# Four reordered steps in a pipelined matmul kernel: a gate transposition placed behind v, u's second half a row further on, the last two results written in four parts

## The chip, the cores and the metric

The kernel runs on one core of one Trainium2 chip. The metric is the device time of one execution in microseconds (us). Before the change the median of three runs is 1119.69 us (1118.13 to 1120.51). The profiled execution took 1119.37 us, and its span, from the first to the last instruction, is 1117.6 us. A difference of less than 0.2% (2.24 us) is about what this kernel's measurement can't tell from no change.

## The reference

Input x is 128 samples of 64 channels by 1024 positions, fp32. Two layers are added to x, one after the other:

- Layer 0: a small network on `cond_128` gives each sample a softmax over 8 experts, so a 64x64 matrix per sample (`agg_w`) and a bias. `x = x + ((agg_w @ x + agg_b) @ (A @ B.T).T + bias)`, with A and B of rank 128.
- Layer 1: a grouped convolution over the 1024 positions (4 groups of 16 channels, 9 taps) with a bias per sample and channel gives y. Then `x = x + y @ W_up.T + delta`, where four gate logits `y @ gate_w.T + expert_bias` choose one expert per row (argmax), and delta is that expert's rank 8 product.

## The kernel before

**Tiles.** Work goes over 32 supertiles (`NS`) of 4 samples, each of two tiles of 128 rows (`NT` = 64), in a software pipeline: the body `for it in range(1, NS)` multiplies supertile `it` by W_up while it prepares `it+1` and `it+2`. Each engine (TensorE is `pe`, ScalarE `act`, VectorE `dve`, the DMA queue of SyncE `sp`) has an order of its own, written out by hand, and they meet at semaphores. fp32 numbers are split into a high and a low fp32r half, and each product is three matmuls (high x high, high x low, low x high).

**Rows.** TensorE's pass has 44 rows, `row(it, n // 4, n % 4)`: 11 blocks of 4 rows with 3 matmuls each (lines 1351 to 1400). Blocks "s" have 384 columns, blocks "c" 292 (the four gate logits, the 32 rank products of the experts and 256 columns of W_up). Between the rows stand the units for the coming supertiles, at fixed places n (lines 1579 to 1622):

- `unit_u(s, h)`: 12 matmuls, x transposed times B, half h at a time, into PSUM tile F[2]. It waits for the low half of x from VectorE (`txl`, line 799). The second half stands behind row 9.
- `unit_tu`: two transpositions of u, behind row 11. ScalarE copies u out of PSUM before it (`ut`) and behind it (`tuu`).
- `unit_v`: u times the samples' matrices, in plain fp32, behind row 13. VectorE adds the bias (`vv`), ScalarE and VectorE split v (`vhi`, `vlo`).
- `unit_p(s, g)` and `unit_c(s, g)`: the convolution. p for g = 0 and 1 is written into PSUM tile M[2], behind rows 15 and 18; ScalarE adds the bias and spreads it (`pc`), and c adds to it.
- `unit_o`: layer 0's last product, four parts, rows 22 to 27.
- `unit_zt(t)`: one transposition (96x128) of the chosen expert's products, `zs`. For the first tile of a supertile (t even) it goes into M[2], behind row 21, for the second into G, behind row 38. ScalarE copies the result into `zst` (`zt`, line 589), and `unit_dl` multiplies it (rows 24 and 28, and row 41). `zs` is made by VectorE in seven small operations (`zc`, lines 961 to 983) once block 2, rows 8 to 11, is complete.

**Who waits for what around the change.** ScalarE's order in a pass is ... h4, ut, tuu, vhi, pc(0), pc(1), bias(0), zt, bias(1) ...; VectorE's is S4, l12, txl, lC, xs, zc, vv, vlo, addU, lB, ty(0) .... In the order of SyncE's queue a pass stores tiles 2it-1 and 2it-2, loads two tiles, copies `Xr`, then loads `xTr` when u's second half is done (line 274), loads `agg` when v is done (296) and `agb` when `vv` is done (287), and so on.

**The end.** `v_f` counts VectorE's six final additions of a supertile, in this order: f11 and fG (rows 0 to 4 of the first tile's 8), f22 and fH (rows 3 to 7 of the second), f21 (rows 0 to 2 of the second), f12 (rows 5 to 7 of the first). A `store` (line 350) writes a tile of 516 KB in one transfer, after `v_f` 5 for the second tile, after 6 for the first. The same `store` closes the kernel (lines 410 and 411).

Of the kernel before, what the change touches and what calls it, by code (L numbers as in the profile page):

```python
# [11 lines left out]
NS = 32  # L12
NT = 64
# [10 lines left out]
XR = 6  # L24
# [8 lines left out]
def adaln_ffn(nc, xT, xP, mlp, wkx, Bd, Ad, biasP, ccT, fsX, Td, Wcd, Wsd, Ld, ebias, out):  # L33
# [10 lines left out]
    with ctx:  # L44
# [3 lines left out]
        def sb(name, shape, dt=fp32):  # L48
            size = 4
            for n in shape[1:]:  # L50
                size *= n
            place[name] = place[""]
            place[""] += (size + 31) // 32 * 32
            assert place[""] <= nc.sbuf_usable_end, (name, place[""], nc.sbuf_usable_end)
            return nc.alloc_sbuf_tensor_at(name, shape, dt, offset=place[name])
# [42 lines left out]
        x1 = sb("x1", [128, XR, 8, 129])  # L98
# [64 lines left out]
        def sem(name):  # L163
            return ctx.enter_context(nc.semaphore(name))
# [9 lines left out]
        d_st = [sem(f"d_st{j}") for j in range(XR)]  # L174
# [4 lines left out]
        a_txh, a_u, a_tu, a_vh, a_xr, a_xs, a_bi, a_pc, a_yh, a_cp, a_zt = (  # L179
            sem(n) for n in ("a_txh", "a_u", "a_tu", "a_vh", "a_xr", "a_xs", "a_bi", "a_pc", "a_yh", "a_cp", "a_zt"))  # L180
        v_mlp, v_wk, v_ag, v_agb, v_b, v_cs, v_a, v_t, v_cb, v_l, v_wc, v_tt, v_w = (
            sem(n) for n in ("v_mlp", "v_wk", "v_ag", "v_agb", "v_b", "v_cs", "v_a", "v_t", "v_cb", "v_l", "v_wc", "v_tt", "v_w"))
        v_txl, v_v, v_vl, v_x1, v_d, v_xr, v_xs, v_ty, v_s, v_yl, v_ux, v_z, v_f = (
            sem(n) for n in ("v_txl", "v_v", "v_vl", "v_x1", "v_d", "v_xr", "v_xs", "v_ty", "v_s", "v_yl", "v_ux", "v_z", "v_f"))
# [76 lines left out]
        def _(sp):  # L261
# [88 lines left out]
            def store(t):  # L350
                s, q = t // 2, t % 2
                sp.wait_ge(v_f, 6 * s + (6 if q == 0 else 5))
                sp.dma_start(out[t], x1[:, t % XR]).then_inc(d_st[t % XR], 16)

            sp.dma_start(pack, mlp).then_inc(d_mlp, 16)
            sp.dma_start(wkr[:, :], wkx).then_inc(d_wk, 16)
            load_xT(0, 0)
# [41 lines left out]
            for it in range(1, NS):  # L399
# [7 lines left out]
                load_agb(it + 3)  # L407
                rx(it + 2, 0)
                load_xT(it + 3, 1)
            store(NT - 1)  # L410
            store(NT - 2)
            for j in range(XR):
                sp.wait_ge(d_st[j], 16 * ((NT - 1 - j) // XR + 1))

        @block.gpsimd
        def _(pool):
# [19 lines left out]
        def _(act):  # L436
            def copy(dst, src):
                return act.activation(dst, src, ACT.Copy)  # L438
# [21 lines left out]
            def tuu(s):  # L460
                if s >= NS:
                    return
                act.wait_ge(p_tu, s + 1)
                copy(u[:, :], F[2][:, 0:256]).then_inc(a_tu, 1)

            def vhi(s):
                if s >= NS:
                    return
                act.wait_ge(v_v, s + 1)
                copy(vh[:, :, :, :, :].rearrange("p q g b n -> p b (q g) n"),  # L470
                     v[:, :].rearrange("p (b g n) -> p b g n", b=4, g=4)).then_inc(a_vh, 1)
# [92 lines left out]
            def h4(s):  # L564
                act.wait_ge(v_s, 4 * s + 4)
                copy(yh[:, 6], yr[:, 6]).then_inc(a_yh, 1)
# [22 lines left out]
            def zt(t):  # L589
                act.wait_ge(p_zt, t + 1)  # L590
                copy(zst[:, :], (M[2] if t % 2 == 0 else G)[0:96, 0:128]).then_inc(a_zt, 1)
# [174 lines left out]
            for it in range(1, NS):  # L766
                txh(it + 2, 1)
                cpGH(it)
                xs(it + 1, 0)
                cpAB(it)  # L770
                h4(it)
                ut(it + 2)
                tuu(it + 2)
                vhi(it + 2)
                pc(it + 1, 0)
                pc(it + 1, 1)
                bias(it + 2, 0)
                zt(2 * it)
                bias(it + 2, 1)
                xsr(it + 1)  # L780
                bias(it + 2, 2)
                xsd(it + 1)
                bias(it + 2, 3)
                hA(it + 1)
                txh(it + 3, 0)
                pc(it + 1, 2)
                cpCD(it)
                pc(it + 1, 3)
                zt(2 * it + 1)
                hB(it + 1)  # L790
                hC(it + 1)
# [463 lines left out]
        def _(pe):  # L1255
# [25 lines left out]
            def unit_v(s):  # L1281
                if s >= NS:
                    return
                pe.wait_ge(a_tu, s + 1)
                pe.wait_ge(d_gg, 32 * s + 64 + 32 * min(s, 1))
                pe.matmul(F[2][:, 0:128], u[:, 0:128], agg[:, 0, :], start=True, stop=True)  # L1286
                pe.matmul(F[2][:, 128:256], u[:, 128:256], agg[:, 1, :], start=True, stop=True).then_inc(p_v, 1)  # L1287
# [16 lines left out]
            def unit_p(s, g):  # L1304
                if s >= NS:
                    return
                if g % 2 == 0:
                    if s == 0:
                        pe.wait_ge(v_xr, g // 2 + 1)
                    else:  # L1310
                        pe.wait_ge(v_xs, 2 * s + g // 2 + 1)
                if s == 0:
                    if g == 0:
                        pe.wait_ge(v_t, 2)
                        pe.wait_ge(v_cs, 1)
                    if g == 1:
                        pe.wait_ge(v_cb, 4)
                    if g > 1:
                        pe.wait_ge(a_pc, 1 if g == 2 else 3)
                elif g == 0:  # L1320
                    if s == 1:
                        pe.wait_ge(a_pc, 4)
                    else:
                        pe.wait_ge(v_f, 6 * (s - 2) + 5)
                elif g == 2:
                    pe.wait_ge(v_v, min(s + 2, NS))
                else:
                    pe.wait_ge(a_pc, 4 * s + g)
                b0 = 4 * (g % 2)
                q = g // 2  # L1330
                for n_, (w, m) in enumerate(((Th, XH(s, q)), (Tl, XH(s, q)), (Th, XL(s, q)))):
                    last = pe.matmul(pbank(s, g)[:, 0:256], w[:, g, 2, :], m[:, 2, b0:b0 + 4, :].rearrange("p b i -> p (b i)"),  # L1332
                                     start=n_ == 0, stop=n_ == 2)
                last.then_inc(p_p, 1)
# [67 lines left out]
            def unit_zt(t):  # L1402
                pe.wait_ge(v_z, 7 * t + 7)
                s = t // 2
                if t % 2 == 0:
                    pe.wait_ge(a_pc, 4 * min(s + 1, NS - 1) + (2 if s + 1 < NS else 4))
                    if s > 0:
                        pe.wait_ge(v_f, 6 * (s - 1) + 5)
                else:
                    pe.wait_ge(v_f, 6 * s + 2)  # L1410
                pe.transpose((M[2] if t % 2 == 0 else G)[0:96, 0:128], zs[:, :], ident[:, :]).then_inc(p_zt, 1)
# [167 lines left out]
            for it in range(1, NS):  # L1579
                for n in range(44):  # L1580
                    row(it, n // 4, n % 4)
                    if n == 9:
                        unit_u(it + 2, 1)
                    if n == 11:
                        unit_tu(it + 2)
                    if n == 13:
                        unit_v(it + 2)
                    if n == 15:
                        unit_p(it + 1, 0)
                    if n == 18:  # L1590
                        unit_c(it + 1, 0)
                        unit_p(it + 1, 1)
                    if n == 21:
                        unit_c(it + 1, 1)
                        unit_zt(2 * it)
                    if n == 22:
                        unit_o(it + 2, 0)
                    if n == 23:
                        unit_o(it + 2, 1)
                    if n == 24:  # L1600
                        unit_dl(2 * it, 0)
                        unit_dl(2 * it, 1)
                    if n == 25:
                        unit_o(it + 2, 2)
                    if n == 27:
                        unit_o(it + 2, 3)
                    if n == 28:
                        unit_dl(2 * it, 2)
                    if n == 30:
                        unit_p(it + 1, 2)  # L1610
                    if n == 34:
                        unit_c(it + 1, 2)
                        unit_p(it + 1, 3)
                    if n == 37:
                        unit_c(it + 1, 3)
                    if n == 38:
                        unit_zt(2 * it + 1)
                    if n == 40:
                        unit_u(it + 3, 0)
                    if n == 41:  # L1620
                        for c in (2, 1, 0):
                            unit_dl(2 * it + 1, c)
# [61 lines left out]
```

## Time and profile before

| | |
|---|---|
| median of 3 runs | 1119.69 us |
| profiled execution | 1119.37 us |
| its span | 1117.6 us |
| TensorE matmul busy | 1085.9 us, 97% of the span |
| VectorE busy | 911.1 us, 82% |
| ScalarE busy | 613.5 us, 55% |
| mean granted TensorE clock | 0.990 |
| DMA, mean over the span | 136 GB/s |

A busy share tells how much of the span an engine had an instruction under way. A matmul's record is longer than the time that it keeps the next one waiting, since they are pipelined; the distance between two starts is what one costs. A weight load (PEld) comes ahead of its matmul, beside the matmul before it. Each row of a timeline is: start in us from the span's start, duration in us, engine, line of the kernel, operation, destination and sources, shape, and in brackets the idle time before it and what ended that. The clock is a share of full speed.

### The profile page before, as it was taken

To read this page: it belongs to the slowest core of one execution; us is meant where nothing else is said; L and a number is where in the kernel's file an instruction comes from. 1 tells how busy PE (TensorE), PEld (TensorE's weight loads), DVE (VectorE), ACT (ScalarE), POOL (GpSimd) and SP (SyncE) were. 2 spreads that over 40 slices of the span, in tenths; PEclk is the share of its full clock that TensorE was granted. 3 is DMA by queue.
4 is the path that set the end of the run, shared out by engine and by line. 5 is a ranking of instruction groups with operands and counts; after the bars stand their busy time and mean duration, and the time that the engine had idled before them with its cause. 6 is when DMAs were issued, how large, how long until landed. Compare 5 with 4: busy or idle time off the path is not lost.

```text
span 1117.6 us, 19137 instructions
## 1 busy us (share of the span) xinstructions
PE 1085.9 (97%) x7020; PEld 1052.2 (94%) x7020; DVE 911.1 (82%) x1670; ACT 613.5 (55%) x1243; POOL 4.5 (0%) x17
## 2 busy tenths in 40 slices
PE   6599999999999999999999999999999999999998
PEld 4478999999999999999999999999999999999998
DVE  5899788888878878878888887887887887888774
ACT  5675555545555555555655555554555555555541
POOL 1000000000000000000000000000000000000000
PEclk9699999999999999999999999999999999999999
DMA  8844455554445554445554454555445555544321
GB/s 317 268 71 135 117 119 151 149 141 138 116 106 153 143 159 128 122 120 128 146 153 138 137 119 104 154 146 151 132 118 114 142 144 156 132 136 121 83 58 76
DMA packets 118048, 152.03 MB, mean 136 GB/s; under 512 B 21836, under 2 KB 91980, under 8 KB 117804
## 3 DMA queue, kind: packets, MB, share of 16 engines
q1 hardware_dynamic: 116516, 148.49, 49.4%
q10 hardware_dynamic: 1440, 2.33, 0.6%
q8 instruction: 56, 0.92, 0.3%
q14 instruction: 36, 0.29, 0.1%
HBM read 80.87 MB, written 35.95 MB: 105 GB/s over the span
## 4 chain that ended last, share of the span: by engine, by line
PE 91%; DVE 4%; DMA 2%; issue 1%; SPq 1%; ACT 1%; DVEq 0%; ACTq 0%
PE M L1398 41%; PE H L1398 9%; PE G L1398 9%; PE F L1347 8%; PE F L1299 7%; PE F L1269 3%; PE F L1271 3%; PE F L1270 3%; PE F L1332 2%; PE M L1332 2%; PE M L1429 2%; DMA Br<-in_Bd_dram 1%; PE F L1287 1%; PE F L1286 1%; DMA Xr<-x 1%
## 5 line engine op out<-in xcount | busy, mean ns | idle before, releaser
L1398 PE MATMUL M<-Wsh,yh 128*128 128x384 f32 x896 | 313.1, 349 | 0.4 <-DVE yl L939 0.4
L1398 PE MATMUL M<-Wsh,yl 128*128 128x384 f32 x896 | 302.9, 338 | 0.0
L1398 PE MATMUL M<-Wsl,yh 128*128 128x384 f32 x896 | 302.9, 338 | 0.0
L888 DVE STREAM_TRANSPOSE yr<-F 128x512 f32<-128x512 f32 x126 | 90.2, 716 | 128.9 <-PE F L1347 80.7
L1398 PEld LDWEIGHTS M<-Wsh,yh 128*128 128x128 f32 x896 | 168.6, 188 | 5.6 <-DVE yl L939 0.7
L1398 PEld LDWEIGHTS M<-Wsl,yh 128*128 128x128 f32 x896 | 168.9, 188 | 2.8
L1398 PEld LDWEIGHTS M<-Wsh,yl 128*128 128x128 f32 x896 | 168.2, 188 | 0.0
L438 ACT ACTIVATE yh<-yr 128x1024 fp32r<-128x1024 f32 (+1 forms) x127 | 120.2, 946 | 53.6 <-DVE yr L903 41.4
L539 ACT ACTIVATE F<-F,cbX 128x128 f32<-128x128 f32 x248 | 69.0, 341 | 94.9 <-PE F L1332 94.1
L539 ACT ACTIVATE F<-M,cbX 128x128 f32<-128x128 f32 x260 | 72.4, 342 | 66.1 <-PE M L1332 66.0
L438 ACT ACTIVATE xTh<-xTr 128x1024 fp32r<-128x1024 f32 x64 | 67.3, 1052 | 61.7 <-DMA xTr<-in_xT_dram 61.7
L438 ACT ACTIVATE F<-biasb 128x512 f32<-128x512 f32 x124 | 74.1, 598 | 25.2 <-DVE yr L888 19.1
L831 DVE TENSOR_TENSOR x<-F,x 128x512 f32<-128x512 f32 x124 | 82.4, 685 | 3.9 <-PE F L1299 0.2
L799 DVE TENSOR_TENSOR xTl<-xTr,xTh 128x1024 fp32r<-128x1024 f32 x64 | 77.8, 1218 | 0.4 <-ACT xTh L438 0.3
L1398 PE MATMUL G<-Wch,yh 128*128 128x292 f32 x256 | 76.3, 298 | 1.1 <-ACT H L438 0.8
L1398 PE MATMUL H<-Wcl,yh 128*128 128x292 f32 x256 | 76.2, 297 | 0.0
L1398 PE MATMUL G<-Wcl,yh 128*128 128x292 f32 x256 | 76.1, 297 | 0.0
L1398 PE MATMUL G<-Wch,yl 128*128 128x292 f32 x256 | 76.1, 297 | 0.0
L1398 PE MATMUL H<-Wch,yl 128*128 128x292 f32 x256 | 76.1, 297 | 0.0
L1398 PE MATMUL H<-Wch,yh 128*128 128x292 f32 x256 | 75.9, 297 | 0.0
L865 DVE TENSOR_TENSOR Xl<-Xd,Xh 128x1024 fp32r<-128x1024 f32 x62 | 75.5, 1218 | 0.0
L1347 PE MATMUL F<-Xh,Th 128*128 128x256 f32 x256 | 73.7, 288 | 1.1 <-DVE Xl L873 0.9
(206 smaller groups left out, 2478.0 us busy)
## 6 DMA issues: line engine op xcount, KB each, us to landing
x<-in_xP_dram SPq DMA_DIRECT2D x64, 516.0 KB, 4.2
out_dram<-x SPq DMA_DIRECT2D x64, 516.0 KB, 3.5
xTr<-in_xT_dram SPq DMA_DIRECT2D x64, 512.0 KB, 4.0
Xr<-x SPq DMA_DIRECT2D x508, 64.5 KB, 2.5
agb<-agb_scratch SPq DMA_DIRECT2D x31, 128.0 KB, 3.5
agg_scratch<-stage SPq DMA_DIRECT2D x1, 2048.0 KB, 9.1
agg<-agg_scratch SPq DMA_DIRECT2D x60, 32.0 KB, 3.3
Wsr<-in_Wsd_dram SPq DMA_DIRECT2D x2, 768.0 KB, 11.0
```

The costliest lines, as they stand in the source:

```text
L438: return act.activation(dst, src, ACT.Copy)
L539: last = act.activation(F[g % 2][:, 128 * b:128 * b + 128].rearrange("p (e i) -> p e i", e=2), pbank(s, g)[:, 64 * b:64 * b + 64].unsqueez ...
L799: dve.tensor_tensor(xl(s, h)[:, :, :], xsrc(s, h)[:, :, :], xh(s, h)[:, :, :].bitcast(fp32), ALU.subtract).then_inc(v_txl, 1)
L831: dve.tensor_tensor(dst, obank(s, i)[:, :].rearrange("p (c a) -> p c a", c=4), dst, ALU.add).then_inc(v_x1, 1)
L865: dve.tensor_tensor(l_[:, 0:2], d_[:, 0:2], h_[:, 0:2].bitcast(fp32), ALU.subtract).then_inc(v_xs, 1)
L888: dve.transpose(dst.rearrange("p j k m -> p (j k) m").rearrange("p (k r) (g b n) -> p g b k r n", r=2, g=2, b=4)[:, g % 2], F[g % 2][:, :] ...
L1269: pe.matmul(F[2][:, 0:256], Bh[:, 4 * h + c, :], xh(s, h)[:, c, :], start=first, stop=False)
L1270: pe.matmul(F[2][:, 0:256], Bh[:, 4 * h + c, :], xl(s, h)[:, c, :], start=False, stop=False)
L1299: last = pe.matmul(obank(s, i)[:, :], w[:, q].rearrange("p g b n -> p (g b n)"), m[:, 4 * h:4 * h + 4, :].rearrange("p c a -> p (c a)"), s ...
L1332: last = pe.matmul(pbank(s, g)[:, 0:256], w[:, g, 2, :], m[:, 2, b0:b0 + 4, :].rearrange("p b i -> p (b i)"), start=n_ == 0, stop=n_ == 2)
L1347: last = pe.matmul(dst[:, e], w[:, g, e, :], m[:, e, b0:b0 + 4, :], start=False, stop=n_ == 2, skip_group_check=True)
L1398: last = pe.matmul(dst, w[:, y, k, :], m, start=fresh and n_ == 0, stop=k == 3 and n_ == 2, skip_group_check=True)
```

## The change

On TensorE u's second half moves from behind row 9 to behind row 10, u's transposition from behind row 11 to behind row 12, v from behind row 13 to behind row 14. `unit_zt(2 * it)`, which was behind row 21, now follows v directly. So it stands ahead of `unit_p(it + 1, 0)`, which writes the same PSUM tile M[2]; it no longer waits for ScalarE's `pc`, and `unit_p(s, 0)` now waits for ScalarE's copy of that transposition (`a_zt`, 2s-1) in place of `v_f`. On ScalarE `zt(2 * it)` moves from behind `bias(it + 2, 0)` to between `tuu` and `vhi`. On SyncE the two last stores become four: rows 0 to 4 of tile 62 after fG (`v_f` 2), rows 3 to 7 of tile 63 after fH (4), rows 0 to 2 of tile 63 after f21 (5), rows 5 to 7 of tile 62 after f12 (6).

```diff
@@ -351,6 +351,10 @@
                 s, q = t // 2, t % 2
                 sp.wait_ge(v_f, 6 * s + (6 if q == 0 else 5))
                 sp.dma_start(out[t], x1[:, t % XR]).then_inc(d_st[t % XR], 16)
+
+            def last_store(t, r0, r1, n):
+                sp.wait_ge(v_f, 6 * (NS - 1) + n)
+                sp.dma_start(out[t][:, r0:r1, :], x1[:, t % XR, r0:r1, :]).then_inc(d_st[t % XR], 16)
 
             sp.dma_start(pack, mlp).then_inc(d_mlp, 16)
             sp.dma_start(wkr[:, :], wkx).then_inc(d_wk, 16)
@@ -407,10 +411,13 @@
                 load_agb(it + 3)
                 rx(it + 2, 0)
                 load_xT(it + 3, 1)
-            store(NT - 1)
-            store(NT - 2)
+
+            last_store(NT - 2, 0, 5, 2)
+            last_store(NT - 1, 3, 8, 4)
+            last_store(NT - 1, 0, 3, 5)
+            last_store(NT - 2, 5, 8, 6)
             for j in range(XR):
-                sp.wait_ge(d_st[j], 16 * ((NT - 1 - j) // XR + 1))
+                sp.wait_ge(d_st[j], 16 * ((NT - 1 - j) // XR + (2 if j in ((NT - 1) % XR, (NT - 2) % XR) else 1)))
 
         @block.gpsimd
         def _(pool):
@@ -771,11 +778,11 @@
                 h4(it)
                 ut(it + 2)
                 tuu(it + 2)
+                zt(2 * it)
                 vhi(it + 2)
                 pc(it + 1, 0)
                 pc(it + 1, 1)
                 bias(it + 2, 0)
-                zt(2 * it)
                 bias(it + 2, 1)
                 xsr(it + 1)
                 bias(it + 2, 2)
@@ -1321,7 +1328,7 @@
                     if s == 1:
                         pe.wait_ge(a_pc, 4)
                     else:
-                        pe.wait_ge(v_f, 6 * (s - 2) + 5)
+                        pe.wait_ge(a_zt, 2 * s - 1)
                 elif g == 2:
                     pe.wait_ge(v_v, min(s + 2, NS))
                 else:
@@ -1402,10 +1409,10 @@
             def unit_zt(t):
                 pe.wait_ge(v_z, 7 * t + 7)
                 s = t // 2
-                if t % 2 == 0:
-                    pe.wait_ge(a_pc, 4 * min(s + 1, NS - 1) + (2 if s + 1 < NS else 4))
-                    if s > 0:
-                        pe.wait_ge(v_f, 6 * (s - 1) + 5)
+                if t == 0:
+                    pe.wait_ge(a_pc, 6)
+                elif t % 2 == 0:
+                    pe.wait_ge(v_f, 6 * (s - 1) + 5)
                 else:
                     pe.wait_ge(v_f, 6 * s + 2)
                 pe.transpose((M[2] if t % 2 == 0 else G)[0:96, 0:128], zs[:, :], ident[:, :]).then_inc(p_zt, 1)
@@ -1579,12 +1586,13 @@
             for it in range(1, NS):
                 for n in range(44):
                     row(it, n // 4, n % 4)
-                    if n == 9:
+                    if n == 10:
                         unit_u(it + 2, 1)
-                    if n == 11:
+                    if n == 12:
                         unit_tu(it + 2)
-                    if n == 13:
+                    if n == 14:
                         unit_v(it + 2)
+                        unit_zt(2 * it)
                     if n == 15:
                         unit_p(it + 1, 0)
                     if n == 18:
@@ -1592,7 +1600,6 @@
                         unit_p(it + 1, 1)
                     if n == 21:
                         unit_c(it + 1, 1)
-                        unit_zt(2 * it)
                     if n == 22:
                         unit_o(it + 2, 0)
                     if n == 23:
```

## Rows read from the trace of the kernel before

**Rows 1.** The page, part 1: busy time of each engine.

```profile
PE 1085.9 (97%) x7020; PEld 1052.2 (94%) x7020; DVE 911.1 (82%) x1670; ACT 613.5 (55%) x1243; POOL 4.5 (0%) x17
```

**Rows 2.** Windows of TensorE: stretch, length, PE busy (x), PEclk, DMA share, GB/s.

```profile
1000.00:1050.00 50.00, 50.00 (x330) 1.00 0.49 132
```

**Rows 3.** Timeline of one pass: u's first half's start, then its second half's.

```profile
696.20 0.28 PE L1269 MATMUL F<-xTh,Bh 128*128 128x256 f32 x1
696.32 0.28 PE L1270 MATMUL F<-xTl,Bh 128*128 128x256 f32 x1
...
702.86 1.22 DVE L799 TENSOR_TENSOR xTl<-xTr,xTh 128x1024 fp32r<-128x1024 f32 x1
...
704.14 0.19 PEld L1269 LDWEIGHTS F<-xTh,Bh 128*128 128x128 f32 x1
704.20 0.33 PE L1269 MATMUL F<-xTh,Bh 128*128 128x256 f32 x1
...
704.37 0.28 PE L1270 MATMUL F<-xTl,Bh 128*128 128x256 f32 x1
```

**Rows 4.** The same pass's timeline: v, the end of zc, the next row.

```profile
707.76 0.38 PE L1286 MATMUL F<-agg,u 128*128 128x128 f32 x2
...
708.22 0.19 DVE L983 TENSOR_TENSOR zs<-zm,zs 128x32 fp32r<-128x32 f32 x1
...
708.38 0.34 PE L1398 MATMUL M<-Wsl,yh 128*128 128x384 f32 x1
```

**Rows 5.** The same pass's timeline: zt, ScalarE's copy, the row behind, the next unit.

```profile
714.58 0.27 PE L1411 MATMUL M<-ident,zs 128*96 128x128 f32 x1
...
714.87 0.34 PE L1398 MATMUL M<-Wsl,yh 128*128 128x384 f32 x1
...
714.89 0.27 ACT L438 ACTIVATE zst<-M 96x128 fp32r<-96x128 f32 x1 [0.53 <-PE M L1411]
...
715.23 0.40 PE L1299 MATMUL F<-Ah,vh 128*128 128x512 f32 x1
```

**Rows 6.** Timeline: three places where TensorE waits for another engine's copy.

```profile
26.73 0.38 ACT L438 ACTIVATE u<-F 128x256 f32<-128x256 f32 x1 [4.33 <-PE F L1271]
...
27.16 0.14 PEld L1278 LDWEIGHTS F<-ident,u 128*128 128x128 f32 x1 [0.68 <-ACT u L438]
...
106.90 0.40 ACT L438 ACTIVATE H<-G 128x292 f32<-128x292 f32 x1
...
107.41 0.19 PEld L1398 LDWEIGHTS G<-Wch,yh 128*128 128x128 f32 x1 [1.06 <-DVE yl L933]
...
1063.96 0.19 PEld L1398 LDWEIGHTS M<-Wsh,yh 128*128 128x128 f32 x1 [0.25 <-DVE x L1014]
...
1064.24 0.34 PE L1398 MATMUL M<-Wsl,yh 128*128 128x384 f32 x1
```

**Rows 7.** Timeline of the last two passes: row 15's start and zc's end.

```profile
1069.80 0.34 PE L1398 MATMUL M<-Wsh,yh 128*128 128x384 f32 x1
...
1070.57 0.19 DVE L983 TENSOR_TENSOR zs<-zm,zs 128x32 fp32r<-128x32 f32 x1
...
1097.16 0.19 DVE L983 TENSOR_TENSOR zs<-zm,zs 128x32 fp32r<-128x32 f32 x1
1097.20 0.34 PE L1398 MATMUL M<-Wsh,yh 128*128 128x384 f32 x1
```

**Rows 8.** Timeline of the end: f12 and the issue of the last two stores.

```profile
1113.14 0.56 DVE L1014 TENSOR_TENSOR x<-M,x 128x384 f32<-128x384 f32 x1
1113.16 0.90 SPq L353 DMA_DIRECT2D out_dram<-x  x2
```

**Rows 9.** Line 353 in 1110 to 1118 us: issue to landing of the last two stores.

```profile
DMA to landing us min/median/max: 2.7/3.0/3.4
```

**Rows 10.** Windows at the end: length, PE, PEld, DVE, ACT, POOL, PEclk, DMA share, GB/s.

```profile
1114.00:1116.40 2.40, 0.00 (x0) 0.00 (x0) 0.00 (x0) 0.00 (x0) 0.00 (x0) 1.00 1.02 409
```

**Rows 11.** The page, part 3: SyncE's DMA queue: packets, MB, share of 16 engines.

```profile
q1 hardware_dynamic: 116516, 148.49, 49.4%
```

## Prediction

> **What bounds the kernel now.** I first read the page's busy shares: TensorE 97% of the span, VectorE 82%, ScalarE 55% [rows 1]. Then the span cut into stretches of 50 us: from 150 us on TensorE is busy throughout and granted the full clock, 2.4 GHz [rows 2]. So the middle of the kernel costs what TensorE's queue costs, and only two things change the time there: matmuls added or removed (the change does neither), and gaps too short to be listed as idle, since the records of pipelined matmuls overlap. These show in the timeline as a distance between two starts above the usual one. Last I read the end, where TensorE is done and the stores are left.
>
> **u's second half a row later: -1.45 us.** In the first half, the second matmul starts 0.12 us after the first. In the second half it starts 0.17 us after, and its weight load is at 704.14, just behind VectorE's xTl, which ends at 702.86 + 1.22 = 704.08 [rows 3]. So TensorE loses 0.05 us here for VectorE. One row more ahead of u is some 0.4 us, far more than that, and VectorE's order up to xTl is not touched, so the gap closes. u's second half exists in 29 passes (it = 1 to 29): 29 x 0.05 = 1.45 us. The bounds are none and 0.06 each, 0 to -1.75.
>
> u's transposition and v keep their distances to u or gain (rows 11 and 12 between them now, 10 and 11 before), so the copies ut and tuu are in time. What is queued behind them comes later: SyncE's load of the next xTr by 0.4 us, those of agg and agb, VectorE's vv and vlo and ScalarE's vhi by 0.5 us. Cover: xTr is copied only at the end of the pass, agg and agb are read in the next one, and vlo has until row 22. Behind vlo, addU has until row 20 and lB until row 24, several rows of 0.5 us later. The copies of Xr that follow in SyncE's queue wait for later additions anyway. I cost these at nothing; if addU's cover were gone, row 20 would wait for what it lacks, in each pass.
>
> **The transposition itself: nothing.** It is only moved. From its start to the second matmul of the row behind are 0.29 us; take off a row matmul's 0.18 and it costs 0.11 [rows 5]. Would it be cheaper right behind v, another plain fp32 product? v is four passes of 128 columns, and takes 708.38 - 707.76 - 0.18 = 0.44 us, again 0.11 each [rows 4]. Passes side by side are no cheaper than one alone, which excludes a gain; and none is dearer, which excludes a loss.
>
> **Does zt wait for zc? In the middle no, in the last two passes yes: +1.4 us.** The new zt starts when row 14 and v are done. Row 14 comes first now (3 x 0.175 = 0.525), then v (0.445): 707.76 + 0.97 = 708.73, less the 0.05 that u no longer loses, 708.68. zs is complete at 708.22 + 0.19 = 708.41 [rows 4], so it is in time by about 0.1 us, with 0.15 to spare for the handover and the weight load. In pass 30 there is no u, tu or v left to fill the rows, but VectorE's work ahead of zc is the same: zc ends at 1070.57 + 0.19 = 1070.76, while zt's place, the start of row 15, is at 1069.80 [rows 7]. With 0.05 for the handover and 0.10 for the weight load (below) zt starts at 1070.91: +1.1 us. In pass 31 zc ends at 1097.35 and row 15 starts at 1097.20 [rows 7]: +0.3. Behind both places TensorE has no slack that could take it up. Bounds: with a quicker load 0.95 and 0.2, and with zt's 0.11 lost once more because a later wait keeps its place, 1.2 and 0.4; 1.15 to 1.6.
>
> **p now waits for ScalarE's copy of zt: +2.7 us.** This is the wait that the change adds. Behind zt stands one row, then unit_p(it+1, 0), which must not overwrite M[2] before ScalarE has copied. Today's zt gives the times: the copy starts 0.31 us after zt's start (714.89 - 714.58) and takes 0.27, so it ends at 0.58; the unit behind the next row starts at 715.23, 0.65 after zt [rows 5]. ScalarE is free (tuu is long done). Where TensorE waited for such a copy into SBUF, its weight load came at 27.16, 0.05 behind 26.73 + 0.38 [rows 6]: 0.63. And a matmul whose load was held starts about 0.10 later: the row at 1063.96 has its second matmul at 1064.24, so the first counts as from 1064.24 - 0.18 = 1064.06 [rows 6]. That makes 0.73 instead of 0.65, or by the row lengths (0.11 + 0.525) instead of 0.64: a hold of 0.08 to 0.10, I take 0.09. There are 30 (it = 1 to 30): 2.7 us. Lower bound: nothing, if only the matmul waits and its weights are loaded ahead, since 0.63 is before 0.65. Upper bound: the load at 107.41 came 0.11 behind ScalarE's copy (106.90 + 0.40) [rows 6], which makes the hold 0.15 and the sum 4.5. The nearest row is the 0.05 of a copy to SBUF, as zst is. Queued behind p are all later rows; ScalarE's pc and TensorE's c follow p at unchanged distances. The Trainium skill, in TensorE: Matmul & The Clock Gate, "Step-by-step: what each phase is for", says that TensorE pulls weight loads ahead of matmuls under way, so that the next weights load beside them; by that the hold would be nothing and the whole 2.7 us less. The row at 1063.96 speaks against it where a wait is in front: that wait protects a PSUM tile only, and the load still came behind it.
>
> **The four last stores: -1.0 us.** Now f21's store goes out at 1113.16 and f12's at about 1113.72 [rows 8]. The latter lands 3.4 us after its issue (the longer of the two) [rows 9], at 1117.1. The two hold 2 x 128 x 4128 bytes, 1.06 MB, which at 409 GB/s [rows 10] take 2.6 us; so 1.4 us are left between the first issue and the landing that no data fills. A lone store agrees: the shorter of the two lands after 2.7 us [rows 9], 1.3 of data and 1.4 beside. After the change 5 rows of tile 62 leave some 10 us earlier, under the rows. Behind fH, done about 0.5 us before 1113.14, 5 rows of tile 63 follow, then 3 rows (0.2 MB) after f21 and 3 after f12: 11 rows of 16, 0.73 MB, 1.8 us. From an issue at 1112.7, with the 1.4, the end is 1115.9: -1.2. Shorter packets cost more: the queue's 116516 packets of 1.27 KB took 0.494 x 1117.6 x 16 = 8833 us, 76 ns each [rows 11], against 161 ns for 4128 bytes at 409 GB/s [rows 10]; on the line between these a packet of 1548 bytes takes 84 ns and one of 2580 bytes 115, eight per engine: 0.9 + 0.7 + 0.7 = 2.3 us, end at 1116.4: -0.7. I take -1.0. The issues on SyncE's queue, about 0.35 us each, fit between the additions. Bounds: 0 (completion is what takes the time) and -1.5 (the last part alone, 1113.72 + 1.4 + 0.5). By the Trainium skill, DMA: Bandwidth & Descriptors, "Anatomy of one DMA", a transfer costs some 2.0 us fixed plus its bytes at 436 GB/s, an estimate of 2.45 us for the last part by which this term would be -0.95; that page's "Bandwidth" also advises batches of 1 MiB or more, against splitting.
>
> **The sum:** -1.45 + 1.4 + 2.7 - 1.0 = +1.65 us. Against the profiled execution's 1119.37 (1.8 us more than its span) that is 1121.0 us. This execution stands 0.3 us under the median of 1119.69.
>
> **The rivals.**
> - *p is not held.* Weights are loaded ahead and the copy is in time. For it: 0.63 against 0.65. Against it: the load behind 1063.96. 1121.0 - 2.7 = 1118.3, still no change that can be told.
> - *The handover from ScalarE takes 0.11 us, and the kernel gets slower.* Place: the same p, in 30 passes; price 0.15 each, 4.5 instead of 2.7: 1122.8 us. It decides from a hold of about 0.11 each, where the sum passes +2.24. For it: 107.41. Against: that copy writes PSUM, and 27.16.
> - *The stores bring nothing,* completion bound: 1122.0.
> - *zt comes too early in each pass,* its slack of 0.1 us being eaten: with 0.1 more in 29 passes, 1123.9. Against it: zc's time repeats to a few hundredths.
>
> **How the numbers follow.** My forecast 0.55, p not held 0.14, a longer handover 0.17, stores without gain 0.08, zt too early 0.06. The range goes from p not held to the longer handover: 1118.3 to 1122.8 us. Over 0.2% faster (2.24 us, about what a measurement of this kernel can tell) needs p not held and both other gains at their best: 0.06. Slower takes the handover, half of the last two, and the forecast's upper edge: 0.28. The rest, 0.66, is no change.
>
> **What would show it.** In the changed profile: u's second half with 0.12 between its first two matmuls; the weight load of p at zt's start + 0.63, p's matmul 0.08 to 0.10 late, and M L1332 waiting on ScalarE's zst; TensorE waiting some 1.1 us before zt near 1070 us and 0.3 near 1097; SyncE's last issue landing under 3 us. Wrong would be: p's load beside the row ahead of it, zt waiting in middle passes, or row 20 waiting for addU.

## The result and the profile after

The changed kernel takes 1123.01 us, the median of 7 runs (1122.29 to 1125.26), beside 1119.45 us for the kernel before (7 runs, 1117.78 to 1120.51): ratio 1.0037, 95% interval 1.0026 to 1.0049. It is slower by 3 to 5.5 us. The forecast was 1121.0 us with a range to 1122.8. The profiled execution took 1122.56 us, its span is 1120.8 us.

The page, part 1, of the changed kernel (before: [rows 1]):

```profile
PE 1089.4 (97%) x7020; PEld 1047.7 (93%) x7020; DVE 912.2 (81%) x1670; ACT 613.5 (55%) x1243; POOL 4.3 (0%) x17
```

The shares hardly differ. What differs is the length of a pass: zt of the second tile stands behind row 38 in both kernels, so the distance between two of them is one pass. Timeline of TensorE, that transposition at the start and the end of the same four passes, the kernel before:

```profile
728.12 0.27 PE L1411 MATMUL G<-ident,zs 128*96 128x128 f32 x1
...
860.46 0.28 PE L1411 MATMUL G<-ident,zs 128*96 128x128 f32 x1
```

and the changed kernel:

```profile
728.73 0.27 PE L1418 MATMUL G<-ident,zs 128*96 128x128 f32 x1
...
861.55 0.27 PE L1418 MATMUL G<-ident,zs 128*96 128x128 f32 x1
```

132.34 / 4 = 33.085 us before, 132.82 / 4 = 33.205 after: +0.12 us a pass. The forecast, -0.05 for u and +0.09 for p, was +0.04. Timeline of one pass of the changed kernel, u's second half first, then zt, its copy, and p:

```profile
705.14 0.28 PE L1276 MATMUL F<-xTh,Bh 128*128 128x256 f32 x1
...
705.26 0.28 PE L1277 MATMUL F<-xTl,Bh 128*128 128x256 f32 x1
...
708.80 0.19 DVE L990 TENSOR_TENSOR zs<-zm,zs 128x32 fp32r<-128x32 f32 x1
...
709.09 0.13 PEld L1418 LDWEIGHTS M<-ident,zs 128*96 128x96 f32 x1
...
709.20 0.27 PE L1418 MATMUL M<-ident,zs 128*96 128x128 f32 x1
...
709.51 0.27 ACT L445 ACTIVATE zst<-M 96x128 fp32r<-96x128 f32 x1 [1.23 <-PE M L1418]
...
709.90 0.19 PEld L1339 LDWEIGHTS M<-Xh,Th 128*128 128x128 f32 x1 [0.22 <-issue]
...
709.93 0.36 PE L1339 MATMUL M<-Xh,Th 128*128 128x256 f32 x1
...
710.12 0.28 PE L1339 MATMUL M<-Xh,Tl 128*128 128x256 f32 x1
```

u's second matmul comes 0.12 us after the first: the gap of [rows 3] is closed. zs is ready at 708.99, and zt's weights load at 709.09, beside v and 0.11 ahead of zt, at v's own pace, so zt waits for nothing. The copy starts 0.31 us after zt and ends at 709.78, 0.58 after it, as in [rows 5]. But p's weight load comes only at 709.90, 0.12 us behind that end where I took 0.05, and p's second matmul shows it starting as from 710.12 - 0.12 = 710.00, 0.80 after zt in place of 0.64. The hold is 0.16 to 0.17 us.

The last two passes, timeline of zc's end and zt (before: [rows 7]):

```profile
1072.98 0.19 DVE L990 TENSOR_TENSOR zs<-zm,zs 128x32 fp32r<-128x32 f32 x1
...
1073.22 0.12 PEld L1418 LDWEIGHTS M<-ident,zs 128*96 128x96 f32 x1 [1.18 <-DVE zs L990]
...
1100.91 0.19 DVE L990 TENSOR_TENSOR zs<-zm,zs 128x32 fp32r<-128x32 f32 x1
...
1101.16 0.12 PEld L1418 LDWEIGHTS M<-ident,zs 128*96 128x96 f32 x1 [0.37 <-DVE zs L990]
```

zt waits for zc in both. It has two waits too, but here the late one (for zs) stands first, and the load comes 0.05 and 0.06 behind zs (1073.22 - 1073.17, 1101.16 - 1101.10). By the distance of the second tiles' transpositions the two passes take 29.16 and 23.15 us, before 27.81 and 22.91: +1.6 us.

The end, timeline of f12 and the last three issues, then line 357's issue to landing for them, then two windows (columns as in [rows 10]):

```profile
1116.68 1.36 SPq L357 DMA_DIRECT2D out_dram<-x  x3
...
1117.12 0.56 DVE L1021 TENSOR_TENSOR x<-M,x 128x384 f32<-128x384 f32 x1
```

```profile
DMA to landing us min/median/max: 2.2/2.5/2.6
```

```profile
1118.00:1119.00 1.00, 0.00 (x0) 0.00 (x0) 0.00 (x0) 0.00 (x0) 0.00 (x0) 1.00 1.02 378
1119.00:1120.00 1.00, 0.00 (x0) 0.00 (x0) 0.00 (x0) 0.00 (x0) 0.00 (x0) 1.00 0.46 166
```

The last part, 194 KB, lands within 2.6 us of its issue, where the whole tile took 3.4 [rows 9], and the shorter packets run at 378 GB/s in the full stretch shown, not 409 [rows 10]. From the last transposition (1109.66 before, 1113.66 after) to the end of the span are 7.94 us before and 7.14 after: -0.8 us.

The ledger: 29 passes x 0.12 = +3.5, last two passes +1.6, the end -0.8: +4.3 us. The ratio says +4.1, the difference of the medians is 3.6. Two things are not in this ledger, and both vary from execution to execution: the start, since the second tiles' first transposition comes at 96.55 us in this trace and at 98.64 in the one before (96.5 to 98.7 in the twelve traces of this case), and a few longer passes, +1.6 us in this trace and +0.2 before. So the two spans differ by only 3.2 us, and the pass is a better measure than the span.

**Three passes were longer still**, 34.00, 33.40 and 33.80 us. Timeline of ScalarE in the first:

```profile
303.68 1.06 ACT L445 ACTIVATE xTh<-xTr 128x1024 fp32r<-128x1024 f32 x1 [3.27 <-DMA xTr<-in_xT_dram]
304.64 0.39 ACT L445 ACTIVATE H<-G 128x292 f32<-128x292 f32 x1
```

xTr landed late; behind the copy of it on ScalarE stands the copy of G into H, and row 8 waits for that. The DMA view of that stretch (298.80 to 304.00 us) shows an instruction packet among the loads, and the pass before (265.60 to 270.80) shows none:

```profile
q1 hardware_dynamic: 361, 1.36, 69.9%
q8 instruction: 1, 0.02, 1.1%
...
xTr<-in_xT_dram SPq DMA_DIRECT2D x1, 512.0 KB, 4.8
```

```profile
q1 hardware_dynamic: 371, 1.40, 73.7%
...
xTr<-in_xT_dram SPq DMA_DIRECT2D x1, 512.0 KB, 3.6
```

Whether these passes belong to the change is taken up below.

### The profile page after: what moved, and what is told of

It reads as the page before. It is cut to its first block, busy times and chain, and to the rows that moved or that the text cites. A ratio compares the mean times of both kernels' runs of the same rounds, so it can differ in the third digit from the quotient of the medians.

```text
span 1120.8 us, 19139 instructions
## 1 busy us (share of the span) xinstructions
PE 1089.4 (97%) x7020; PEld 1047.7 (93%) x7020; DVE 912.2 (81%) x1670; ACT 613.5 (55%) x1243; POOL 4.3 (0%) x17
## 4 chain that ended last, share of the span: by engine, by line
PE 91%; DVE 5%; DMA 1%; issue 1%; SPq 1%; ACT 1%; DVEq 0%; ACTq 0%
PE M L1405 40%; PE H L1405 9%; PE G L1405 8%; PE F L1354 8%; PE F L1306 7%; PE F L1278 3%; PE F L1276 3%; PE F L1277 3%; PE M L1339 2%; PE F L1339 2%; PE M L1436 2%; DMA xTr<-in_xT_dram 1%; PE F L1294 1%; PE F L1293 1%; DVE wks L1123 0%
```

## The experiments

The theory (A): the move of zt is the whole loss, by p's hold and by zt's wait in the last two passes; u's row and the stores gain what was forecast. Its rival (B): u and v a row later send SyncE's loads later and lose something there. "Before" is each time the kernel before, run on the same chip as the kernels that it is compared with: 1118.48 us for the first four, 1119.19 for the next four, 1118.64 for the last two.

### zt back behind row 21

```diff
                     if n == 14:
                         unit_v(it + 2)
-                        unit_zt(2 * it)
...
                     if n == 21:
                         unit_c(it + 1, 1)
+                        unit_zt(2 * it)
```

and on ScalarE behind bias(0), with the old waits.

> The changed kernel with the even transposition zt back behind row 21 on TensorE and behind bias(0) on ScalarE, with its old waits; u, its transposition, v and the four last stores stay as changed. Theory A (the loss is the zt move: p(it+1,0) held 0.17 us by ScalarE's copy in 30 passes, zt waiting 1.2 us for zc in the last two): the kernel loses all of that, so the steady pass falls from 33.20 to 33.08 - 0.05 = 33.03 us and the time to 1119.4 - 1.5 - 0.8 = 1117.1 us. Rival B (part of the loss comes from u and v a row later, which send SyncE's loads later, so that the xTr load lands late in some passes and holds row 8): passes of 33.2 to 34 us stay, time 1118 to 1119.5.

Measured: 1115.79 us, ratio 0.9978 (0.9969 to 0.9987), faster than before by 1.5 to 3.5 us. Timeline, the same four passes:

```profile
725.51 0.27 PE L1418 MATMUL G<-ident,zs 128*96 128x128 f32 x1
...
857.63 0.27 PE L1418 MATMUL G<-ident,zs 128*96 128x128 f32 x1
```

132.12 / 4 = 33.03 us, 0.055 under the kernel before and 0.175 under the changed one. The last two passes are back at 27.83 and 22.90. Rival B falls: u and v stand a row later here too, and no pass but the first is over 0.1 us longer than the rest. Nor is the load of xTr that row 8 depends on sent later by the change: in all twelve traces it goes out 2.76 to 2.79 us after the second tile's transposition.

### The four stores alone

```diff
-            store(NT - 1)
-            store(NT - 2)
+            last_store(NT - 2, 0, 5, 2)
+            last_store(NT - 1, 3, 8, 4)
+            last_store(NT - 1, 0, 3, 5)
+            last_store(NT - 2, 5, 8, 6)
```

> The kernel before with the four last stores alone. Theory A: the end from TensorE's last transposition to the last instruction shortens from 7.94 to 7.14 us as in the changed kernel, everything else as before: 1119.4 - 0.8 = 1118.6 us. Rival (the end's time is completion of the last transfer, whatever its size): no change, 1119.4.

Measured: 1118.05 us, ratio 0.9996 (0.9987 to 1.0005). The runs alone can't tell 0.8 us from nothing. In the trace the last transposition is at 1107.45 and the span ends at 1114.4: 6.95 us, against 7.94 before, with passes of 33.07 to 33.11. Over all traces this stretch is 7.93 to 7.99 us in the four kernels with two stores and 6.82 to 7.14 in the eight with four parts, on the mean 6.94: the gain is 0.8 to 1.1 us, mostly 1.0. The first experiment less this one is u's move alone: 33.085 - 33.03 = 0.055 us a pass, 1.6 us.

### zt into G

```diff
-                pe.transpose((M[2] if t % 2 == 0 else G)[0:96, 0:128], zs[:, :], ident[:, :]).then_inc(p_zt, 1)
+                pe.transpose((G[0:96, 292:420] if t % 2 == 0 else G[0:96, 0:128]), zs[:, :], ident[:, :]).then_inc(p_zt, 1)
...
-                        pe.wait_ge(a_zt, 2 * s - 1)
+                        pe.wait_ge(v_f, 6 * (s - 2) + 5)
```

ScalarE copies from there. The output of this kernel is wrong: the transposition now stands between the rows that sum into G and the product that is added to that sum (`unit_dl`, row 24), and what it does to the sum was not followed up. The instructions are the same in number and size as in the changed kernel, so it serves for the times alone.

> The changed kernel with the even transposition written into free columns of PSUM tile G in place of M[2], so that p(it+1,0) doesn't wait for ScalarE's copy (it waits for v_f as before). zt stays right behind v. Theory A: p's weight load comes in the row ahead of it again, 0.17 us less in 30 passes: 1123.0 - 5.0 = 1118.0 us, steady pass 33.03 to 33.05 us. Rival C (what holds p is not the copy but something that follows zt, v and one row, such as the wait instruction itself): p's load still about 0.07 us late, steady pass 33.1 to 33.2, time over 1120.

Measured: 1117.43 us, ratio 0.9993 (0.9984 to 1.0002). Timeline of one pass, zt, its copy, p's weight load:

```profile
708.12 0.27 PE L1418 MATMUL G<-ident,zs 128*96 128x128 f32 x1
...
708.43 0.27 ACT L445 ACTIVATE zst<-G 96x128 fp32r<-96x128 f32 x1 [1.23 <-PE G L1418]
...
708.58 0.19 PEld L1339 LDWEIGHTS M<-Xh,Th 128*128 128x128 f32 x1
708.75 0.28 PE L1339 MATMUL M<-Xh,Th 128*128 128x256 f32 x1
```

The load goes beside the row ahead, while the copy still runs, and p starts 0.63 us after zt. The pass is 32.98 to 33.05 us, three late ones aside; the last two, where zt still waits for zc, are 29.01 and 23.15. So it is the wait for the copy that holds p, and zt right behind v costs nothing in the middle passes. The Trainium skill, TensorE: Matmul & The Clock Gate, "Step-by-step: what each phase is for", has weight loads pulled ahead of running matmuls; this trace agrees (0.17 us ahead) where the wait is long met. The changed kernel's trace shows that a late wait keeps the load behind it.

### The order of p's two waits

Why 0.12 us behind the copy, and 0.05 at [rows 6], first pair? p has two waits, for xs (long past) and then for the copy. The load behind u's copy has one. So has the load at 1063.96, the third place of [rows 6]. What it waits for is not a copy but the addition of VectorE below, which ends at 1063.91, so the load is 0.05 behind. The load at 107.41, 0.11 behind its copy, has two again, and the late one is second (lines 1368 and 1369).

```profile
1063.36 0.55 DVE L1014 TENSOR_TENSOR x<-M,x 128x384 f32<-128x384 f32 x1
```

```diff
+                if g == 0 and s > 1:
+                    pe.wait_ge(a_zt, 2 * s - 1)
                 if g % 2 == 0:
...
                     if s == 1:
                         pe.wait_ge(a_pc, 4)
-                    else:
-                        pe.wait_ge(a_zt, 2 * s - 1)
```

> The changed kernel with the two waits ahead of unit_p(s, 0) in the other order: first for ScalarE's copy of zt (the late one), then for v_xs (long past). The weight load came 0.12 us behind the end of the copy in the changed kernel, but 0.05 us behind it where TensorE waits for one thing only (u's copy). Theory D (the handover is longer when the late wait is the second of two): load 0.05 to 0.06 us behind the copy, hold 0.10 instead of 0.17, 30 x 0.07 = 2.1 us less, 1120.9 us. Rival E (0.12 us belongs to this copy of ScalarE): no change, 1123.0 us.

Measured: 1120.49 us, ratio 1.0018 (1.0007 to 1.0030). Timeline:

```profile
743.93 0.27 PE L1418 MATMUL M<-ident,zs 128*96 128x128 f32 x1
...
744.24 0.27 ACT L445 ACTIVATE zst<-M 96x128 fp32r<-96x128 f32 x1 [1.23 <-PE M L1418]
...
744.57 0.19 PEld L1339 LDWEIGHTS M<-Xh,Th 128*128 128x128 f32 x1 [0.16 <-ACT zst L445]
```

The copy ends at 744.51, the load comes 0.06 behind. The pass is 33.12 us (33.09 to 33.14, three late ones aside), 0.09 less than the changed kernel's. Nothing but the order of two waits was changed. Theory D holds here; the hold that is left is 0.10 to 0.11, about the size that I had forecast.

### The last two passes alone

```diff
+                        if it < NS - 2:
+                            unit_zt(2 * it)
...
                         unit_c(it + 1, 1)
+                        if it >= NS - 2:
+                            unit_zt(2 * it)
```

The same on ScalarE, with the old waits where zt stands at its old place.

> The changed kernel, but in the last two passes (it = 30 and 31) the even transposition stands behind row 21 again, with its old waits. Theory A: the last two passes fall from 29.16 and 23.15 us back to 27.83 and 22.90 (1.6 us together), the other passes stay at 33.20 to 33.21: 1.6 us below the changed kernel run beside it. Rival (the last two passes are long because of p's hold or of the late VectorE chain, wherever zt stands): 28.9 or more and 23.1.

Measured: 1122.64 us, ratio 1.0022 (1.0012 to 1.0032). By the trace as theory A has it: last passes 27.80 and 22.90 us, the undisturbed others 33.13 to 33.21, 33.19 in the middle. By the times the step is not resolved: the changed kernel, run beside it (below), took 1122.73. Five passes of this trace are 0.3 to 0.6 us longer, 2.2 us together, each with late xTr, which hides the step.

### A met wait ahead, and behind

Does D hold for VectorE's results, and at another place? In the kernel before, at u's second half:

```diff
+                if s > 2 and h == 1:
+                    pe.wait_ge(v_v, s)
                 pe.wait_ge(v_txl, 2 * s + h + 1)
```

> The kernel before, with a wait that is long met (for v_v, of the pass before) put ahead of the late wait for VectorE's xTl at u's second half, in 29 passes. Nothing else changes. Theory D (a late wait that stands second hands over 0.06 us later, whatever engine it waits for): the weight load moves from 0.06 to 0.12 us behind xTl's end, u's hold grows from 0.05 to 0.11, steady pass 33.15 us, 29 x 0.06 = 1.7 us slower. Rival E (only ScalarE's copies hand over late): no change, 33.09.

> The same added wait, but behind the late one. Theory D: as the kernel before, steady pass 33.09 us, load 0.06 us behind xTl's end. Rival F (each further wait costs TensorE some 0.06 us where it is held, in whatever order): 33.15 us as with the wait ahead.

Measured: ahead 1123.16 us, ratio 1.0032 (1.0023 to 1.0042); behind 1120.38 us, ratio 1.0008 (0.9998 to 1.0018). Timelines of xTl and u's load, ahead:

```profile
704.90 1.23 DVE L799 TENSOR_TENSOR xTl<-xTr,xTh 128x1024 fp32r<-128x1024 f32 x1 [0.48 <-ACT xTh L438]
...
706.24 0.19 PEld L1271 LDWEIGHTS F<-xTh,Bh 128*128 128x128 f32 x1
```

and behind:

```profile
703.31 1.22 DVE L799 TENSOR_TENSOR xTl<-xTr,xTh 128x1024 fp32r<-128x1024 f32 x1
...
704.58 0.19 PEld L1271 LDWEIGHTS F<-xTh,Bh 128*128 128x128 f32 x1
```

0.11 us (706.24 - 706.13) against 0.05 (704.58 - 704.53), and so in all 28 steady passes of the two traces (0.11 to 0.12 against 0.04 to 0.05). The undisturbed passes are 33.16 us in the middle (33.12 to 33.18) against 33.10 (33.06 to 33.11). D holds for VectorE too: E and F fall. Of the loss of the kernel with the wait ahead, 2.6 to 4.7 us by the ratio, 29 x 0.07 = 2.0 us is this steady part. The forecast of 1.7 us left out the late passes: they make 4.2 us in its trace and 0.2 in the trace before.

### The changed kernel again

> The changed kernel once more, for a second trace and beside the kernels of this call. Theory A: steady pass 33.20 to 33.21 us, last two 29.16 and 23.15. The passes in which xTr lands late and holds row 8 (three of 29 in the first trace, 1.4 us) are either chance (other passes or none here) or belong to the kernel (the same three again).

Measured: 1122.73 us, ratio 1.0029 (1.0018 to 1.0040); pass 33.20 us, last two 29.16 and 23.16. The passes it = 2 and 3 were 0.1 and 0.5 us longer, none of the first trace's three (it = 7, 19, 27). So whether one of those is late changes from execution to execution of the same kernel. Which passes can be late does not, as the account of the late passes below shows.

### Two met waits ahead

As the met wait ahead, with a second one, for `v_vl`.

> The kernel before with two long met waits (for v_v and v_vl of the pass before) ahead of the late wait for xTl at u's second half. Theory D1 (only the last wait goes with the weight load itself, and a held one behind others hands over later by one fixed step): as with one met wait, load 0.11 us behind xTl's end, steady pass 33.15 us. Theory D2 (each wait ahead adds its own 0.06 us): load 0.17 behind, 33.21 us.

Measured: 1121.90 us, ratio 1.0028 (1.0013 to 1.0044). xTl ends at 706.60 in the pass looked at and the load comes at 706.72, 0.12 behind; undisturbed passes are 33.12 to 33.17 us. That is theory D1: the step is one of 0.06 us, with two met waits ahead as with one. Four passes of this trace were over 0.4 us longer, again with late xTr, which is why the loss, 1.5 to 4.9 us by the ratio, can be above the 2 us that the step alone makes.

### A kernel that beats both

zt back behind row 21 as in the first experiment, and at row 8:

```diff
-                    pe.wait_ge(v_yl, 5 * s + 2)
                     pe.wait_ge(a_cp, 3 * s + 1)
+                    pe.wait_ge(v_yl, 5 * s + 2)
```

> The changed kernel with zt back behind row 21, and the two waits ahead of block 2 (row 8) exchanged, so that the one that is late when xTr lands late (ScalarE's copy of G into H) comes first. Theory D: steady pass 33.03 us, as with zt back alone, and 0.07 us less in each of the few passes that wait there: 2.5 to 3 us under the kernel before, 1116.3 us if that takes 1119. Rival: the gain seen with zt back alone was that chip's, under 1 us here.

Measured: 1115.61 us, ratio 0.9971 (0.9961 to 0.9982), 2.0 to 4.4 us under the kernel before. Passes are 32.99 to 33.07 us, but for three of 33.5 to 33.9 with late xTr. So late passes come with zt at its old place as well. Timeline of row 8 in one of them, the copy of G into H and the load behind it:

```profile
304.54 0.40 ACT L445 ACTIVATE H<-G 128x292 f32<-128x292 f32 x1
...
304.99 0.19 PEld L1405 LDWEIGHTS G<-Wch,yh 128*128 128x128 f32 x1 [0.61 <-ACT H L445]
```

The load comes 0.05 behind the copy, and 0.05 to 0.06 in each of the four passes of this trace in which it stands idle for it. With the waits in the old order it is 0.10 to 0.12 in every such pass of the other eleven traces (the 107.41 of [rows 6] is one). So D holds at a third place, and for a copy into PSUM. It is worth 4 x 0.06 = 0.2 us here, too little for the times: the first experiment has 0.9978 (0.9969 to 0.9987) without it.

## Why the prediction was wrong

- **u's row: right.** -0.05 a pass forecast, -0.055 shown (33.09 to 33.03), 1.6 us.
- **zt itself, and zt right behind v: right.** It costs the same there, and waits for nothing in the middle passes (third experiment: 33.03 us a pass, as with zt at its old place).
- **zt in the last two passes: right.** +1.4 and p's hold of 0.09 forecast, +1.6 measured. In the third experiment, where p isn't held, zt's waits alone are 29.01 - 27.83 + 23.15 - 22.90 = +1.4. The fifth takes all of it away in the trace.
- **The stores: right.** -1.0 forecast, -0.8 to -1.1 in the traces, too little for the runs to tell.
- **p's hold: the term that was mis-sized.** The mechanism was as described: the copy 0.58 us after zt, the weight load kept behind the wait, the matmul 0.10 after its load. What failed is "the nearest row is the 0.05 of a copy to SBUF". It measured 0.12, the hold 0.17 instead of 0.09, and the sum 30 x 0.17 = 5.0 us instead of 2.7. I chose between the two rows of [rows 6] by where the copy writes. That is not what matters: the copy into PSUM of the second row hands over in 0.05 too once its wait stands first (the last experiment). What matters is whether a met wait stands ahead of the late one, and p's late one is the second. Exchanging two lines brings back 0.06 us of handover, and 0.09 a pass. The rival with 0.11, given a chance of 0.17, was the case, and at 1122.8 its time was 0.2 us under the median. What in the engine makes the order of the waits matter, no run here shows.

With the hold at 5.0 us the sum is -1.45 + 1.4 + 5.0 - 1.0 = +3.95, against +4.1 by the ratio. The range ended where that rival's time stood, with nothing beyond it for the runs' own spread.

The late passes were not in the forecast. They are in traces of both orders of zt, and small ones in the trace before (33.22 and 33.18 us); between none and five to an execution cost over 0.3 us each, up to 1.1. There are 27 of these in the twelve traces, the first pass aside, and their places are not chance: each is a pass it = 3, 7, 11 and so on, every fourth, or, in the three kernels with an added wait, 24 or 28. All 27 had an instruction packet in the stretch between xTr's issue and the copy of it; of the passes without one, none was over 0.2 us late. But another 32 passes had such a packet and lost 0.2 us at most. So the packet's place goes with the program, and whether it costs anything changes from one execution to the next. That the packet is the cause was not tested.

## What to carry to other kernels

When one instruction waits for several things, put the wait that comes last in time first in the program: on TensorE here that was worth 0.06 to 0.09 us each time, some 2 us over a kernel of 30 passes. A transposition moved ahead of the next user of its PSUM tile turns a wait that was long met into one that is late by as much as the copy, the handover and the held weight load together exceed the rows between them; count those three before moving it. And look at the passes in which the pipeline runs empty: what covers a producer in the middle (u, v and their copies) is not there at the end.

## What the runs showed of the hardware

- TensorE's weight load follows the end of the work that it waits for by 0.05 to 0.06 us when that wait is alone or first, and by 0.10 to 0.12 when one or two long met waits stand ahead of it; for ScalarE's results (p and row 8) and VectorE's (u's second half) alike.
- A held weight load starts its matmul 0.10 to 0.11 us later, so a hold begins before any idle time shows: in the changed kernel the profile gives none for p's matmul, only "0.22 <-issue" ahead of the load.
- The last three parts, one of 323 KB and two of 194, landed 2.2 to 2.6 us after their issue, the first of the two whole tiles of 516 KB after 2.7 [rows 9]. The Trainium skill, DMA: Bandwidth & Descriptors, "Anatomy of one DMA", gives some 2.0 us plus the bytes at 436 GB/s for transfers issued from GpSimd, an estimate of 2.45 us for a part of 194 KB. The trace agrees there, though these go out from SyncE. For the whole tile the same sum is an estimate of 3.2 us, and there the measured 2.7 is below it.
